# Moving a residual add from VectorE to identity products on TensorE and a copy on ScalarE, in a two-layer attention and expert kernel

## What is computed

```python
x = x + attention0(groupnorm(x))         # softmax attention, 4 heads of 32, q and k scaled by their norms
t = tokens(x)
t = t + attention1(layernorm(t))         # linear attention: softmax(q), softmax(k), context, w_out, group norm
t = t + experts(layernorm(t))            # router over 8 experts, the best 2 weighted, expert_w[e]
```

## Time and profile before

| | |
|---|---|
| median of 3 runs | 3159.14 us (3149.65 to 3159.78) |
| the profiled execution's own time | 3163.6 us |
| its span | 3161.8 us |
| TensorE busy | 2930.5 us, 93% |
| VectorE busy | 2582.7 us, 82% |
| ScalarE busy | 2437.8 us, 77% |
| GpSimd busy | 705.1 us, 22% |
| mean granted TensorE clock | 0.955 |

### The profile page before, as it was taken

How to read it: one execution, slowest core, us unless ns; L and a number is a source line. 1 busy time by engine, 2 the same in 40 slices (tenths; PEclk the granted TensorE clock), 3 DMA queues, 4 the chain that set the end, 5 groups by cost and what they waited for, 6 DMA issues and landing times.

```text
span 3161.8 us, 62165 instructions
## 1 busy us (share of the span) xinstructions
PE 2930.5 (93%) x20368; PEld 1047.0 (33%) x20368; DVE 2582.7 (82%) x3652; ACT 2437.8 (77%) x3196; POOL 705.1 (22%) x726
## 2 busy tenths in 40 slices
PE   6999999989899999998989999998788999999988
PEld 3222222375322222237532222223743222222474
DVE  4888888877688888887768888888786888888967
ACT  4999999744699999974469999996446999999734
POOL 1122221114312221211421222121152222122115
PEclk8999999988899999998989999999898999999979
DMA  2555565400265555540025555554002555555300
GB/s 85 113 108 108 111 115 97 94 1 19 57 115 107 108 107 107 108 81 1 21 62 108 108 113 110 100 108 80 1 21 45 108 111 108 107 104 110 69 1 27
DMA packets 72168, 257.86 MB, mean 82 GB/s; under 512 B 8160, under 2 KB 10240, under 8 KB 71808
## 3 DMA queue, kind: packets, MB, share of 16 engines
q0 software_dynamic: 64512, 234.91, 39.3%
q1 hardware_dynamic: 7296, 18.51, 1.6%
HBM read 10.12 MB, written 8.39 MB: 6 GB/s over the span
## 4 chain that ended last, share of the span: by engine, by line
PE 75%; issue 11%; DVE 5%; DMA 4%; ACT 4%; POOL 1%; SPq 0%; ACTq 0%; POOLq 0%; DVEq 0%
PE BK L1024 73%; DMA RM<-EA 3%; ACT EA L523 2%; DVE X L997 2%; PE BK L1029 1%; POOL KE L449 1%; ACT KE L523 1%; ACT SMC L527 1%; DVE ST L634 0%; DVE X L989 0%; DVE ST L673 0%; PE BK L1286 0%; DVE RU L627 0%; DVE RU L628 0%; SPq L332 0%
## 5 line engine op out<-in xcount | busy, mean ns | idle before, releaser
L804 DVE TENSOR_TENSOR XT<-XT,KE 128x512 f32<-128x512 f32 x1344 | 1574.5, 1231 | 178.9 <-ACT KE L523 174.9
L523 ACT ACTIVATE KE<-BK 128x512 f32<-128x512 f32 (+1 forms) x1536 | 1486.3, 1023 | 153.8 <-PE BK L1024 75.1
L1024 PE MATMUL BK<-Q,K 32*128 32x512 f32 x8192 | 1184.7, 645 | 54.8 <-ACT SMC L527 22.3
L1024 PE MATMUL BK<-KE,V 128*32 128x512 f32 x6144 | 821.3, 607 | 0.6 <-ACT KE L523 0.6
L408 POOL DMA_DIRECT2D RM<-EA x448 | 392.0, 929 | 1564.1 <-DVE RM L789 398.4
L1024 PEld LDWEIGHTS BK<-Q,K 32*128 32x128 f32 x8192 | 328.5, 184 | 921.0 <-ACT KE L523 657.7
L523 ACT ACTIVATE EA<-BK 128x512 f32<-128x512 f32 (+1 forms) x512 | 499.2, 1021 | 35.5 <-PE BK L1024 3.3
L1024 PEld LDWEIGHTS BK<-KE,V 128*32 128x32 f32 x6144 | 121.4, 108 | 586.0 <-ACT KE L523 386.5
L1024 PE MATMUL BK<-EA,V 128*32 128x512 f32 x2048 | 272.9, 605 | 0.0
L602 ACT ACTIVATE RM<-BK,GT 128x128 f32<-128x128 f32 x512 | 145.9, 368 | 145.0 <-PE BK L1024 144.8
L1024 PE MATMUL BK<-WEXP,XT 128*128 128x512 f32 x512 | 241.6, 619 | 16.4 <-DVE X L997 16.4
(11 more groups left out here) (155 smaller groups left out, 1911.3 us busy)
## 6 DMA issues: line engine op xcount, KB each, us to landing
RM<-EA POOLq DMA_DIRECT2D x224, 768.0 KB, 6.6
RM<-EA POOLq DMA_DIRECT2D x224, 256.0 KB, 3.3
XN<-in_x SPq DMA_DIRECT2D x16, 512.0 KB, 5.8
out<-X SPq DMA_DIRECT2D x16, 512.0 KB, 2.9
WEXP<-in_L_ffn_expert_w SPq DMA_DIRECT2D x1, 512.0 KB, 6.9
CONST<-in_consts SPq DMA_DIRECT2D x1, 384.0 KB, 6.0
WQKV<-in_L_conv_w_qkv SPq DMA_DIRECT2D x1, 192.0 KB, 2.3
WQKV<-in_L_attn_W_qkv SPq DMA_DIRECT2D x1, 192.0 KB, 5.9
```

The source lines that it names most:

```text
L523: nc.scalar.activation(exps(jt, p), scored(c * T + jt, p).rearrange("p a n -> p (a n)"), ACT.Exp, scale=SCALE0).then_inc(s_exp, 1)
L804: v.tensor_tensor(acc, acc, exps(jt, p), ALU.add).then_inc(s_adds, 1)
L1024: return nc.tensor.matmul(o, lhsT, rhs, start=start, stop=stop, skip_group_check=shared)
```

## The change

TensorE first multiplies the identity by a chunk of `X` into the bank (`residual`, one product of 512 columns), and the projection's four products then add to it (`start=False`). ScalarE copies the finished bank over `X` (`onto_x`, eight copies per stage, ahead of its part of the normalising). VectorE's adds are gone; it takes the statistics of what ScalarE wrote. In stage A the merge stands behind the statistics of chunk 0 in VectorE's stream. In stage B seven of the identity products stand ahead of TensorE's wait for `AT2`, the eighth behind chunk 6, and the two averages of the group norm use bank 7 instead of bank 0.

```diff
@@ ScalarE
+                def onto_x(ready, done, chunks):
+                    for c in chunks:
+                        act.wait_ge(ready, b * NCH + c + 1)
+                        part = X[:, c * TPB:(c + 1) * TPB, :].rearrange("p t c -> p (t c)")
+                        nc.scalar.activation(part, BK[c], ACT.Copy).then_inc(done, 1)
...
+                onto_x(s_y0, s_x0, range(NCH - 1))
                 for half in range(2):
                     chunks = range(half * HCH, (half + 1) * HCH)
                     normed(0, half)
                     for c in chunks:
                         keys(c)
                     if half == 0:
+                        onto_x(s_y0, s_x0, [NCH - 1])
                         for c in chunks:
                             values1(c)
...
+                onto_x(s_y2, s_x1, range(NCH))
                 normed(1, 0)
                 normed(1, 1)
@@ VectorE
-                dve.wait_ge(s_bias, b * 4 + 4)
-
-                def onto_x(ready, done, c):
-
-                    dve.wait_ge(ready, b * NCH + c + 1)
-                    part = X[:, c * TPB:(c + 1) * TPB, :].rearrange("p t c -> p (t c)")
-                    v.tensor_tensor(part, BK[c], part, ALU.add).then_inc(done, 1)
-
-                def onto_x_and_normed(ready, done, half):
+
+                def statistics_and_normed(done, half):
 
                     first = half * HCH
                     for c in range(first, first + HCH):
-                        onto_x(ready, done, c)
-                        if c == 1 and ready is s_y0:
+                        if c == 2 and done is s_x0:
                             dve.wait_ge(s_zero, b + 1)
                             merge(b * NCH + NCH, 1, True)
                         if c > first:
...
-                mix_link(v.tensor_copy(SMALL[:, 0:1], BK[0][:, 0:1]))
+                mix_link(v.tensor_copy(SMALL[:, 0:1], BK[7][:, 0:1]))
@@ TensorE
+                def residual(c):
+
+                    part = X[:, c * TPB:(c + 1) * TPB, :].rearrange("p t c -> p (t c)")
+                    mm(BK[c], IDENT, part, stop=False, shared=True)
+
                 def project(c):
+                    residual(c)
                     for t in range(c * TPB, (c + 1) * TPB):
-                        last = mm(BK[c][:, (t % TPB) * C:(t % TPB + 1) * C], Q[:, t * P:(t + 1) * P], WOUT0[:, :])
+                        last = mm(BK[c][:, (t % TPB) * C:(t % TPB + 1) * C], Q[:, t * P:(t + 1) * P], WOUT0[:, :],
+                                  start=False, shared=True)
                     last.then_inc(s_y0, 1)
...
+                for c in range(NCH - 1):
+                    residual(c)
 
                 pe.wait_ge(s_at, b * 3 + 3)
-                tiles(lambda t: QT[:, t * P:(t + 1) * P], lambda t: AT2[:, :], s_y2)
+                for c in range(NCH):
+                    if c == NCH - 1:
+                        residual(c)
+                    for t in range(c * TPB, (c + 1) * TPB):
+                        last = mm(BK[c][:, (t % TPB) * C:(t % TPB + 1) * C], QT[:, t * P:(t + 1) * P], AT2[:, :],
+                                  start=False, shared=True)
+                    last.then_inc(s_y2, 1)
```

More of the change, by code:

```diff
@@ L847, in onto_x_and_normed @@
                     layernorm(mix_link, half, statistics(first + HCH - 1))
-                onto_x_and_normed(s_y0, s_x0, 0)
+                statistics_and_normed(s_x0, 0)
                 dve.sem_inc(s_smc, 1)
                 reciprocals(b * NCH + NCH, s_sum, SM)
-                onto_x_and_normed(s_y0, s_x0, 1)
+                statistics_and_normed(s_x0, 1)
                 def k_maxima(chunks):
@@ L915, in _ @@
                 dve.wait_ge(s_gst, b * 2 + 2)
-                mix_link(v.tensor_scalar(RA[:, 0:1], BK[0][:, 1:2], -1.0, 1e-5, ALU.mult, ALU.add))
+                mix_link(v.tensor_scalar(RA[:, 0:1], BK[7][:, 1:2], -1.0, 1e-5, ALU.mult, ALU.add))
                 rsqrt(mix_link, SMALL[:, 3:4], RA[:, 0:1], 1)
@@ L925, in _ @@
                 for half in range(2):
-                    onto_x_and_normed(s_y2, s_x1, half)
+                    statistics_and_normed(s_x1, half)
                 def over(x2):
@@ L1262, in _ @@
                 pe.wait_ge(s_bst, b * 2 + 1)
-                mm(BK[0][:, 0:1], NEG, MV[:, 0:1]).then_inc(s_gst, 1)
+                mm(BK[7][:, 0:1], NEG, MV[:, 0:1]).then_inc(s_gst, 1)
                 pe.wait_ge(s_bst, b * 2 + 2)
-                mm(BK[0][:, 1:2], NEG, SMALL[:, 2:3]).then_inc(s_gst, 1)
+                mm(BK[7][:, 1:2], NEG, SMALL[:, 2:3]).then_inc(s_gst, 1)
+                for c in range(NCH - 1):
+                    residual(c)
                 pe.wait_ge(s_at, b * 3 + 3)
-                tiles(lambda t: QT[:, t * P:(t + 1) * P], lambda t: AT2[:, :], s_y2)
+                for c in range(NCH):
[5 more added lines that the diff above has]
+                    last.then_inc(s_y2, 1)
                 for half in range(2):
```

## The result

The changed kernel takes 3137.8 us, the median of 6 runs (3132.4 to 3141.4), beside 3157.8 (3149.7 to 3160.7) for 6 runs of the kernel before. The ratio is 0.9934, with a 95% interval of 0.9921 to 0.9948.

The account below looks back on a forecast made before the run. Two short stages in each of four batches, not the long attention, were taken to decide. Stage A 1.6 + stage B 6.4 = 8 us off 3163.6, thus 3155.6; the same share off the median gives 3151 us, range 3139 to 3166.

Parts of the forecast that it names:

- What bounds the kernel: Whole kernel: the edit leaves the long attention alone; one of two short stages in each of four batches decides.
- Prices: Unit costs: identity product 0.86 us at full clock, 1.72 at the lower; chunk of projection 0.89; ScalarE's copy 0.59.
- Stage A, first half: Sums to ScalarE's normalising: 7.05 us for 7.77, so 0.7 gained; in the fourth batch sums start 0.4 late.
- Stage A, second half: `project(7)`: uncovered identity product against an earlier layernorm, +0.68; with the first half +0.5 us in three batches, +0.1 in the fourth.
- Stage B, first half: Up to ScalarE's first normalising: 1.3 us sooner, or 0.4 later where the clock is low before the identity products.
- Stage B, second half: Second layernorm earlier without four adds, useful if router products quicken: 2.5 us in two batches, 0.7 in two.
- rival 2: The clock stays up nearly everywhere: 3.6 us per stage B, 0.4 per stage A, 16 us, 3143 us; chance 0.20.
- The rule on transposes: Sixteen transposes before the router: skill says they don't count as busy, so clock always down there; the trace disagrees.
- The forecast of busy time: TensorE's busy time rises by 64 x 0.86 = 55 us, less where the clock is better.
- the clock gives nothing (1): Stage B: router stays at 6.99, only the first half's gain counts, 1.8 us, with stage A 3.4: 3156 us; chance 0.28.
- Slower (3): Identity products run at the lower clock, 4.7 us late per stage B: 3176 us, or 3164 in two batches; chance 0.14.
- rival 4: VectorE's adds bound more than seen, so most of 42.8 us comes back; chance 0.03.

Follow-up runs that it names:

- experiments 1: The change in stage A alone, stage B as in the kernel before: ratio 0.9978 to the kernel before, median 3150.7 us.
- 5: Changed kernel without stage B's identity products, so the residual is left out there and VectorE has no adds: 0.9955 of the kernel before, 3144.2 us.
- 7: Changed kernel with four, not seven, of stage B's identity products ahead of the wait and ScalarE's last two copies behind its first normalising: 0.9933, 3138.2 us.
- experiment 8: Changed kernel plus thrown-away identity products in TensorE's idle time, four ahead of the key transposes and three in the group norm: 0.9914, 3131.3 us.
- experiment 9: Changed kernel plus two thrown-away identity products among each half's router products, and a wait for all eight chunks: 1.0023 of the kernel before, 3163.0 us.
- experiment 4: Changed kernel with each of stage B's identity products behind the wait for `AT2`, directly ahead of its chunk: 1.0022 of the kernel before, 3163.8 us.
- experiment 6: Changed kernel plus an unused VectorE maximum ahead of each chunk's statistics in stage B: 0.9982 of the kernel before, 3152.4 us.
- experiment 11: Kernel before plus thrown-away products ahead of the `AT2` wait, at the key transposes, in the group norm and among the router products: 1.0016, 3163.0 us.
- experiment 3: Kernel before plus four thrown-away identity products in TensorE's idle time ahead of the wait for `AT2`, no work moved: 0.9984, 3150.7 us.
- the ladder: Stage A's change alone, then also stage B without VectorE's adds or identity products, then the changed kernel: 0.9978, 0.9955, 0.9934 of the kernel before.

## Why the prediction was wrong, point by point

**What bounds the kernel** held: two short stages per batch, and nothing in the attention (593.3 and 593.2 us per batch).

**Prices** held. Fourteen records took 6.25 and the next product started 6.09 behind their start, 0.87 a product (I took 0.86), and the copy takes 0.60.

**Stage A, first half** held: 7.04 or 7.05 from sums to `Z` in all four batches, forecast 7.05, and 7.77 before. That it holds to the hundredth is luck, for the terms that I named add up to 7.00. The 0.30 of the table's first column is less than this 0.72, since the merge landed later on average in the changed kernel's execution.

**Stage A, second half** was right in sign and too small. I charged an uncovered identity product against VectorE's shorter way, 0.5 us gained in three batches and 0.1 in one, and kept the durations round it. Z0 to K is 0.56 us shorter per batch, and in experiments 1, 5, 7, 8 and 9 too (28.76 to 28.77); 4 and 6 have 29.10 and 29.16, and those that leave stage A alone 29.13 to 29.54. Stage A gives 3.4 us by the two columns (4 x 0.30 + 4 x 0.56), where I had 1.6. The clock is behind the 0.56, which had no term. The five microseconds behind the first `Z`, in the kernel before (first batch) and, with the same code in stage A, in experiment 11 (third batch):

```profile
626.30:631.30 5.00, 3.95 (x17) 3.35 (x18) 5.00 (x9) 5.00 (x12) 0.00 (x0) 0.68 0.00 0
```

```profile
2199.82:2204.82 5.00, 3.51 (x19) 2.37 (x20) 5.00 (x9) 5.00 (x13) 0.00 (x0) 1.00 0.00 0
```

From this `Z` to ScalarE's `Z` of the second half it is 14.50 to 15.08 in the kernel before, with the clock at 0.66 to 0.70, and 14.22 to 14.24 in the changed kernel, with 1.00 in all four batches. In that one batch of experiment 11 the old code ran at 1.00, and took 14.25. From there to K all kernels take 14.5. So at one clock the identity product and VectorE's shorter way cancel, about as I had reckoned (0.86 against 0.68), and what the changed kernel gains here is the clock.

**Stage B, first half** was right in kind. Batch 1 gains 1.07 us (forecast 1.3), and the second, whose identity products took 7.66, loses 0.13 (forecast 0.4), because the clock was down before they began, as I had said. But I gave that case to two batches and it came in one; the others gained 1.1 to 1.5: 3.5 us for 1.8.

**Stage B, second half** is the step that failed, by the size of its term: "I take 2.5 us, between 1.3 and 3.6, in two batches and 0.7, between -0.4 and 1.9, in two." Less the first half's part, that is 4.6 us of the sum. Measured is 11.04 to 8.64 from Z2 to Z3, in every batch, 9.6 us, and another 3.9 from Z3 to the router's end, 13.5 in all. The mechanism was the right one: VectorE's relief is of use only with faster router products, and experiment 3 shows the other side of it, faster router products with Z2 to Z3 at 11.04 still. Two parts of the size were wrong. The helpful case came in four batches and not in two: the router's first half takes 4.93, 5.55, 5.18 and 5.02 us, for 6.99 in each. And its second half was given no gain at all ("The router, the experts and the attention keep their own durations"), though its 4.15 was read from the first batch alone: in the four batches it took 4.15, 6.99, 4.08 and 6.99, and takes 3.91, 4.88, 4.41 and 4.07. From Z2 to the router's end the batches gain 2.5, 4.0, 1.7 and 5.2, the most where the second half had been at the lower clock. It is rival 2, "the clock stays up nearly everywhere", at 3143, that came nearest, and I gave it 0.20.

**The rule on transposes.** The clock isn't always down at the router, as it would be if transposes counted for nothing: in the changed kernel it stays at 1.00 from 699 to 705, where TensorE does little but the sixteen transposes. Before, it was at 0.51 from 703 to 709, with the same sixteen. So they didn't decide it alone, and what did isn't settled.

**What had no term at all**: 3.3 us from K to the averages and 2.1 us in the experts, where nothing was moved. "The router, the experts and the attention keep their own durations" is false for the first two. In experiment 8, where the idle time ahead of the keys is filled, K to avg is 29.14 in every batch, so the clock can do this; in the changed kernel one batch has 29.14 and three 30.7. Some of it may be chance: the experts range from 74.17 to 75.58 in executions that share their code, and the profiled execution of before lay 5.8 us above its median, which these columns share in.

**The forecast of busy time** "rises by 64 x 0.86 = 55, less where the clock is better" was my own warning: it rose by 6.0. With 64.1 us of identity products in it, the rest of TensorE's work got 58 us shorter. The 135 us less at the lower clock would make it 67, an estimate from the mean clocks. Most of that isn't on the path, but my sum had almost none of it.

**Rivals.** That the clock gives nothing (1) is refuted by experiment 3, by its interval and by 7.41 for 9.74; the step from 5 to the changed kernel points the same way. Slower (3) needs identity products at the lower clock; in the changed kernel that came only as 7.66 in one batch, in experiment 8 as 7.95 or near it in all four, and with the order changed in experiment 4. Experiment 6 shows that VectorE's relief is real, and its 14.6 us are far from the 42.8 of rival 4.

**Open** is the exact split. By the ladder it is some 7 us of stage A, 7 us of VectorE's relief in stage B and 6.6 us of identity products that keep the clock, the first good to some 4 us and the others to some 7. In stage A the traces separate the two: per batch 0.72 behind the sums, which is the moved work (before, the fourth batch's sums took 1.07 too, and its `Z` came 7.77 behind their start as in the others), and 0.56 between the first `Z` and K, which is the clock; that is 5.1 us in four batches, and 0.35 less for a batch whose merge lands early, since TensorE's added products then outlast the wait (the sums start 7.13 behind the attention in such batches of experiments 4 to 7 and 9, where it was 6.78). In stage B VectorE's relief and the clock need each other (3, 5 and 6), so no split of them is to be had there.

## What to carry to other kernels

In this kernel work that went to TensorE cost less than nothing, dense, in an idle time and ahead of the wait. In another, look at the stretches with their granted clock behind each idle time, and price what stands there at either level. Here the order of the same instructions (experiment 4) was worth 26 us and the moved work 20, so where an added product stands is the first question and its duration the second. And ask who is next to bind: faster router products gave 0.3 of their 2.4 us while VectorE's adds stood behind them (3). A clock gain in one place was given back in the next in 7 and, from K to R, in 8, so such a gain has to be timed as a whole.

## What the runs showed of the hardware that I had not expected

- The granted clock can be the lower one while TensorE is busy. In experiment 9 TensorE shows as busy for 100% of 707.2 to 711.0 and of 711.0 to 714.0, with 128x512 products among the router's in the first of them, and the granted clock was 0.50 in both. In the kernel before, 709 to 716 was 96% busy with router products at 0.50.
- A dense stretch moved a fall of the clock into the next stage instead of sparing it: in the changed kernel from the transposes (703 to 709 at 0.51 before) to the router products (705 to 710 at 0.73), and in experiment 8 to the identity products of stage B (7.95 for 6.25).
- Less time at the lower clock was not less time: the twelve timings of experiment 9 have mean clocks of 0.970 to 0.973, those of before beside them 0.954 to 0.962, and its median is 5.6 us higher. The products that it adds are part of that, and so is where they stand: the router's products, all on the path, run at 0.50.
